# The end of a fused attention and gated-MLP kernel: a residual moved among additions, a projection ordered by tiles, the last tile normalised on VectorE

## The reference, cut to what matters

```python
Q, K, V = x @ wq.T, x @ wk.T, x @ wv.T                       # 64 wide, no softmax
energy  = V^T K summed over the tokens                        # a 64 x 64 matrix
x = layernorm(x + (Q @ energy^T * sqrt(3/64)) @ wo.T)         # 256 wide
h = silu((x @ w1.T) * s1) * ((x @ w2.T) * s2)                 # 1024 wide
h = gelu((h @ h1.T) * hs1)                                    # exact gelu, 1024 x 1024
h = gelu((h @ h2.T) * hs2)                                    # exact gelu, 1024 x 1024
x = layernorm(x + (h @ w3.T) * s3)                            # 256 wide: the output
```

## Time and profile before

| | |
|---|---|
| median of three runs | 668.91 us (667.25 to 669.6) |
| the profiled execution's own time | 669.32 us |
| its span, first to last instruction | 667.5 us |
| TensorE busy | 645.5 us (97%) |
| VectorE busy | 472.5 us (71%) |
| ScalarE busy | 402.9 us (60%) |
| GpSimd busy | 278.1 us (42%) |
| mean granted TensorE clock | 0.989 of full speed |

### The profile page before, as it was taken

How to read it: one execution, slowest core, us unless ns; L and a number is a source line. 1 busy time by engine, 2 the same in 40 slices (tenths; PEclk the granted TensorE clock), 3 DMA queues, 4 the chain that set the end, 5 groups by cost and what they waited for, 6 DMA issues and landing times.

```text
span 667.5 us, 9250 instructions
## 1 busy us (share of the span) xinstructions
PE 645.5 (97%) x3217; PEld 542.1 (81%) x3217; DVE 472.5 (71%) x704; ACT 402.9 (60%) x684; POOL 278.1 (42%) x229
## 2 busy tenths in 40 slices
PE   8988999979999999999999999999999999999994
PEld 6957788858878888888888888888888888888893
DVE  1257557898655799588855799588755799488456
ACT  1366779846764466655764466655764466666663
POOL 0346599569000267059000267059000267078034
PEclk9999999979999999999999999999999999999997
DMA  8999896944340005734340015734340015444101
GB/s 314 402 363 316 325 367 237 358 184 142 135 167 1 1 14 184 275 127 141 133 169 1 1 19 179 275 127 143 135 163 1 0 24 193 162 144 172 64 1 65
DMA packets 24370, 103.89 MB, mean 156 GB/s; under 512 B 2224, under 2 KB 3312, under 8 KB 16496
## 3 DMA queue, kind: packets, MB, share of 16 engines
q1 hardware_dynamic: 24320, 103.24, 43.9%
HBM read 87.51 MB, written 23.07 MB: 166 GB/s over the span
## 4 chain that ended last, share of the span: by engine, by line
PE 82%; POOL 6%; DMA 4%; DVE 3%; ACT 3%; issue 2%; SPq 1%; POOLq 0%; ACTq 0%; DVEq 0%
PE ps L1219 55%; PE ps L1167 17%; PE ps L1277 8%; DMA w_dram<-in_w2T 2%; DMA w<-w_dram 1%; ACT junk L541 1%; PE ps L1106 1%; POOL quarter L496 1%; POOL quarter L499 1%; POOL beside L424 1%; POOL unit L426 1%; POOL unit L428 1%; POOL unit L430 1%; PE ps L1094 1%; ACT R L627 1%
## 5 line engine op out<-in xcount | busy, mean ns | idle before, releaser
L1219 PE MATMUL ps<-R,ring 128*128 128x512 f32 x1792 | 412.0, 391 | 2.2 <-issue 1.3
L1219 PEld LDWEIGHTS ps<-R,ring 128*128 128x128 f32 x1792 | 337.0, 189 | 73.2 <-issue 2.0
L869 DVE TENSOR_TENSOR R<-quarter,R 128x512 fp32r<-128x512 f32 x284 | 256.4, 924 | 68.5 <-ACT R L627 68.2
L627 ACT CAST R<-quarter 128x512 fp32r<-128x512 f32 x288 | 175.5, 616 | 27.1 <-POOL quarter L499 10.0
L1167 PE MATMUL ps<-x1T,w 128*128 128x512 f32 x512 | 119.7, 392 | 2.3 <-DVE quarter L863 2.0
L1167 PEld LDWEIGHTS ps<-x1T,w 128*128 128x128 f32 x512 | 95.3, 188 | 24.5 <-DVE quarter L863 2.4
L673 ACT ACTIVATE quarter<-U,sc 128x512 f32<-128x512 f32 x96 | 69.5, 724 | 71.8 <-DVE U L888 31.6
L477 POOL TENSOR_TENSOR quarter<-quarter,quarter 128x512 f32<-128x512 f32 x32 | 49.4, 1543 | 99.8 <-ACT quarter L673 92.1
L435 POOL TENSOR_TENSOR ve<-mv,eps 128x4 f32<-128x4 f32 x14 | 5.2, 371 | 197.8 <-DVE mv L846 197.8
L593 ACT ACTIVATE sg<-ps,sc 128x512 f32<-128x512 f32 x64 | 44.1, 690 | 66.2 <-PE ps L1167 66.0
L643 ACT COPY U<-ps 128x512 f32<-128x512 f32 x96 | 56.2, 586 | 39.8 <-PE ps L1219 39.7
(11 more groups left out here) (74 smaller groups left out, 344.9 us busy)
## 6 DMA issues: line engine op xcount, KB each, us to landing
ring<-combos SPq DMA_DIRECT2D x56, 1024.0 KB, 4.9
combos<-unit SPq DMA_DIRECT2D x8, 1024.0 KB, 6.3
unit<-in_h1T SPq DMA_DIRECT2D x4, 1024.0 KB, 15.2
xr<-in_x_rows SPq DMA_DIRECT2D x8, 512.0 KB, 5.7
unit<-in_h2T SPq DMA_DIRECT2D x4, 1024.0 KB, 6.9
xT<-in_xT SPq DMA_DIRECT2D x7, 512.0 KB, 8.1
out<-xr SPq DMA_DIRECT2D x7, 512.0 KB, 2.9
w<-w_dram SPq DMA_DIRECT2D x3, 1024.0 KB, 9.4
```

Source lines behind the costliest of these rows:

```text
L627: nc.scalar.copy(R[slot_of(p, u)][:, 0, c, :], quarter[operand_home(p, u)][:, c, :]).then_inc(hi_done, 1)
L869: nc.vector.tensor_tensor(r[:, 1, c, :], quarter[operand_home(p, u)][:, c, :], r[:, 0, c, :].bitcast(f32), ALU.subtract).then_inc(lo_done, 1)
L1219: last = nc.tensor.matmul(ps[:, bank + j, :], w, view(R[slot_of(p, u)][:, part, k, :]), start=n in (0, 1, 5) and k == 0 and part == 0, sto ...
```

## The change

1. VectorE: `residual2(6)` moves ahead of `add_third` 0 in the last hidden layer. `stats` of block 6 is split: bn_stats of tiles 0 and 1 behind add 0, bn_stats of tiles 2 and 3 and all four bn_aggr behind add 1 (ahead of lo 0).
2. TensorE: block 7's 64 matmuls are ordered by tile. With (use, tile): (16,0), (16,1), (16,2), (17,0), (16,3), (17,1), (17,2), (17,3), eight matmuls each. The waits for the additions are set at each tile that needs one, and the four `lo_tail` waits all stand in (16,0), the four `lo_done` waits of use 17 all in (17,0).
3. The last tile of block 7 is normalised by VectorE, as (y - mean) * rstd in one instruction; GpSimd makes no shift for it, and its store waits for the new semaphore `last_norm`.
4. GpSimd makes the shift of block 7's other tiles in one instruction (mean * rstd * -1) in place of two with a wait between them.

```diff
# SyncE
             for q in range(TPB):
-                sp.wait_ge(tile_norm[1], q + 1)
+                sp.wait_ge(*((tile_norm[1], q + 1) if q < TPB - 1 else (last_norm, 1)))
# GpSimd
+            def shift_of_block():
+                nc.gpsimd.tensor_tensor(shift[:, 0, :], mv[1][:, 0, :, 0], nones[:, :], ALU.mult).then_inc(shift_half, 1)
+                pool.wait_ge(shift_half, 1)
+                pool.wait_ge(rstd_done[1], NB - 1)
+                nc.gpsimd.tensor_tensor(shift[:, 0, :], shift[:, 0, :], rstd[1][:, 0, :], ALU.mult).then_inc(shift_done, 1)
+            def shift_of_tile(q):
+                pool.wait_ge(tile_rstd[1], q + 1)
+                nc.gpsimd.tensor_scalar(shift[:, 1, q:q + 1], mv[1][:, 1, q, 0:1], rstd[1][:, 1, q:q + 1], -1.0,
+                                        ALU.mult, ALU.mult).then_inc(shift_done, 1)
...
-                    if ln == 1:
-                        shift_of(slice(q, q + 1), 1, q + 2)
+                    if ln == 1 and q < TPB - 1:
+                        shift_of_tile(q)
# ScalarE
-            for q in range(TPB):
+            for q in range(TPB - 1):
                 normalise_tile(NB - 1, q, q + 2, tile_norm[1])
# VectorE, in the hidden layers
+                if l == 1 and not more:
+                    residual2(NB - 2)
                 for j in range(KH + 1):
...
                     if j < KH:
                         add_third(L, j)
+                    if l == 1 and not more and j < 2:
+                        stats(1, NB - 2, NB - 1, (range(2), range(2, TPB))[j])
# VectorE, in normalised_tilewise
                 if ln == 0:
                     for q in range(early, TPB):
                         normalise_tile(q)
+                else:
+                    normalise_tile(TPB - 1)
...
-            residual2(NB - 2)
-            stats(1, NB - 2, NB - 1)
             normalised_tilewise(1, NB - 1, down_residual, 1)
# TensorE
+            def w3_last(view):
+                p, L = NP - 1, 2 * NP - 1
+                def tile(u, q):
+                    first = u == 16
+                    slot, at = R[slot_of(p, u)], KH if first else 0
+                    if first:
+                        pe.wait_ge(*((gelu_done, n_gelu(L, 1, 2 + q)) if q < 2 else (add_done, n_add(L, 2, q - 2))))
+                    for k in range(KH):
+                        if q == 0:
+                            pe.wait_ge(*((lo_tail, k + 1) if first else (lo_done, n_split(p, 16, k))))
+                        for part in range(2):
+                            last = nc.tensor.matmul(tail_rows(q), view(slot[:, part, k, q * P:(q + 1) * P]), view(w3[:, at + k, :]),
+                                                    start=first and k == 0 and part == 0, stop=not first and k == KH - 1 and part == 1,
+                                                    skip_group_check=True)
+                    if not first:
+                        last.then_inc(w3b, 1)
+                for u, q in ((16, 0), (16, 1), (16, 2), (17, 0), (16, 3), (17, 1), (17, 2), (17, 3)):
+                    tile(u, q)
...
-                        w3_half(NB - 1, 0, view)
-                        w3_half(NB - 1, 1, view)
+                        w3_last(view)
```

More of the change, by code:

```diff
@@ L195, in build @@
         norm_done = [sem(f"norm_done{i}") for i in range(2)]
-        tail_norm = sem("tail_norm")
+        tail_norm, last_norm = sem("tail_norm"), sem("last_norm")
         tile_scaled = sem("tile_scaled")
@@ L526, in _ @@
                 inverse_deviation(1, 2 * p + 1)
-            shift_of(slice(0, TPB), 0, 1)
+            shift_of_block()
             inverse_deviation_tilewise(1)
@@ L831, in residual2, with stats @@
                                         ALU.add).then_inc(sum_done[1], 1)
-            def stats(ln, b, n):
+            def stats(ln, b, n, tiles=range(TPB)):
                 y = xr[:, b % 4, :].rearrange("p (t e) -> p t e", e=E)
@@ L840, in stats @@
                     dve.wait_ge(tile_norm[0], TPB)
-                for q in range(TPB):
+                for q in tiles:
                     last = nc.vector.bn_stats(st[ln][:, b % 2, q, :], y[:, q, :])
+                if tiles[-1] < TPB - 1:
+                    return
                 last.then_inc(stats_done[ln], 1)
@@ L969, in normalise_tile @@
                     nc.vector.tensor_scalar(y[:, q, :], y[:, q, :], mv[ln][:, ln, q, 0:1], rstd[ln][:, ln, q:q + 1],
-                                            ALU.subtract, ALU.mult).then_inc(tile_norm[ln], 1)
+                                            ALU.subtract, ALU.mult).then_inc(tile_norm[0] if ln == 0 else last_norm, 1)
                 for q in range(TPB):
@@ L1259, in w3_half @@
                         pe.wait_ge(gelu_done, n_gelu(2 * p + 1, 1, j))
[L1260 to L1275, removed]
+                for k in range(KH):
+                    pe.wait_ge(lo_done, n_split(p, u, k))
+                    w = view(w3[:, at + k, :])
+                    for q in range(TPB):
                         for part in range(2):
-                            last = nc.tensor.matmul(tail_rows(q) if b == NB - 1 else rows_of(b)[:, q, :], view(slot[:, part, k, q * P:(q + 1) * P]), w,
-                                                    start=first and k == 0 and part == 0 and (q % 2 == 0 or b == NB - 1),
+                            last = nc.tensor.matmul(rows_of(b)[:, q, :], view(slot[:, part, k, q * P:(q + 1) * P]), w,
+                                                    start=first and k == 0 and part == 0 and q % 2 == 0,
                                                     stop=not first and k == KH - 1 and part == 1, skip_group_check=True)
-                    if tail:
-                        last.then_inc(w3b, 1)
                 if u == 15:
@@ L1285, in w3_half @@
                     last.then_inc(w3c, 1)
-                if u == 17 and not tail:
+                if u == 17:
                     last.then_inc(w3b, 1)
+            def w3_last(view):
[5 more added lines that the diff above has]
+                        pe.wait_ge(*((gelu_done, n_gelu(L, 1, 2 + q)) if q < 2 else (add_done, n_add(L, 2, q - 2))))
+                    for k in range(KH):
+                        if q == 0:
[8 more added lines that the diff above has]
+                    tile(u, q)
             pe.wait_ge(zeros_made, 1)
```

## The result

| | before | after |
|---|---|---|
| median of 14 runs | 668.88 us (667.18 to 672.88) | 665.93 us (664.32 to 667.25) |
| ratio, after to before | | 0.9952, 95% interval 0.9937 to 0.9967 |
| profiled span | 667.5 us | 664.4 us |
| first matmul of product 6 (L1219, now L1231) | 642.55 | 642.32 |
| end of the last normalisation | 665.35 | 662.20 |

The change gains 2.95 us by the medians; 2.86 were forecast (665.93 measured, 666.05 predicted). By the interval of the ratio the gain is between 2.2 and 4.2 us. The two executions shown already differ by 0.23 us ahead of product 6, where nothing was changed, so from here on times with a plus sign count from the first matmul of product 6. By that clock the last normalisation ended at +22.80 us before and ends at +19.88 us after, and the span at +24.95 and +22.08.

What follows compares the result with a forecast made beforehand. VectorE's serial queue plus a chain of small steps was taken to bound the end. Last bn_aggr at 661.15, plus 1.34 and 2.15, gives 664.64 against 667.50, 2.86 less; from the median 668.91 that is 666.05 us, range 664.8 to 667.9.

Steps and rivals of the forecast that it cites:

- What bounds it: End of the kernel: VectorE's serial queue plus a chain of small steps; VectorE time lost ahead of 661.44 comes off one for one.
- Part 1: Block 6's residual and statistics moved on VectorE: 4.16 us of work, 1.85 us of cover; lo 3 runs 1.17 us later.
- rival C: VectorE's queue, 644 to 650: all moved work ahead of lo 0 held beside GpSimd; slower, 670.1 us; chance 0.04.
- A (no hold): Waits at operands shared by GpSimd and VectorE don't arise; lo 3 ends 652.9 to 653.5, total 665.3 us; chance 0.22.
- B (further holds): More moved VectorE work held, or slow shift and store landing: gain 1.5, 667.4 us; chance 0.16 together with D.
- Rival D: Tile (16,0) on TensorE waits for `lo_tail` 3 if L444 ends after 650.4; each further 0.5 costs 0.5; 0.16 with B.
- Part 2: Last projection by tiles: TensorE stands 0.90 us for lo 3, first tile ready at 654.81; new order costs 0.4 us.
- Parts 3 and 4: Last tile's steps and GpSimd's shift: 1.34 us from last bn_aggr to normalisation's end in place of 2.39, a gain of 1.05.
- The sum: Whole change: span ends at 664.64 against 667.50, 2.86 us less; from the median, 666.05 us.

Runs made afterwards that it cites:

- e2: Kernel before with only TensorE's new order of the last 64 matmuls; last normalisation at +22.80 us as before, ratio to before 1.0000.
- e1: Kernel before with only block 6's residual and statistics moved; last normalisation at +20.17 us against +22.80, ratio to before 0.9954.
- e6: Full change, but GpSimd's four L444 wait until block 6's residual sum is written; sum takes 1.23 us, last normalisation at +19.89 against +19.88.
- e4: Full change with the old order of the 64 matmuls; last normalisation at +19.53 us against the full change's +19.88, ratio to before 0.9949.
- the repeat: The full change run once more against the kernel before; last normalisation again at +19.88 us, ratio to before 0.9967.
- e5: Full change with tile (16,3) put behind (17,2); last normalisation at +19.41 us against the full change's +19.88, ratio to before 0.9953.
- e7: Full change with block 6's later statistics spread into gaps of VectorE; last normalisation at +19.17 us against the full change's +19.88, ratio to before 0.9952.
- e3: Kernel before with only VectorE's last-tile normalisation and the one-instruction shift; last normalisation at +21.82 us against +22.80, ratio to before 0.9978.

## Why the prediction was right

Step by step, in the prediction's order; predicted times are its own less the 0.23 us by which this execution was ahead.

- **What bounds it.** VectorE's queue ahead of the first tile set the end. e2 shows that TensorE's order alone is worth nothing, e1 that the move is worth 2.63 us of 2.92.
- **Part 1.** The sum L836 was to be held until GpSimd's first instruction ends: about 1.85 us, measured 1.87; lo 0 about 1.35, measured 1.36; lo 3 to end at 653.87, measured 653.88. The bn_stats and additions beside GpSimd were charged nothing, and took 0.74 us a pair and 0.68, against rival C. e6 turns the cause on and off. Rivals A (no hold) and B (further holds) fall with these rows. Rival D's wait for `lo_tail` did not arise: the last L444 ended at 649.32, 0.8 us ahead of need; e6 shows what it looks like when it does.
- **Part 2.** The stop at chunk 3 of (17,0) was put at 0.90 us and cost 0.84 (8.67 - 7.83). It was worked out for the weight load, taken to run 0.22 us ahead of its matmul; after the wait both are recorded at 653.93, so the 31st matmul itself is only 0.73 late, and the 34 from there take 4.34 us, 0.11 more than 30 (3.75) and four more at 0.12. The tiles came 0.08 to 0.11 us earlier than forecast. That the new order costs 0.4 us was forecast and is 0.35 (e4).
- **Parts 3 and 4.** The steps took 1.35 us against 1.34 forecast. The shift that no row had shown took 0.26 us (0.37 in the first tile), inside the bounds given. Two readings were not right. GpSimd was to have 0.6 us of slack for the last tile, and had none to speak of: its rstd instruction took 0.83 and 0.82 us in the middle tiles in place of 0.55 (see the last section), and its last shift ended at 660.94, as the last tile's step was due at 660.93. A tile took GpSimd 1.44 us (659.49 to 660.93) where 1.1 was forecast, against VectorE's 1.45. It cost nothing: GpSimd began 0.08 us after the bn_aggr, as it did in the first tile, when it was idle (656.04 to 656.12). And of the 1.05 us that the prediction books under the last steps, 0.41 are the move's: in e1 GpSimd takes up the last tile 0.11 us after its bn_aggr, not 0.52, with the old shift still in place. By then the steps are worth 0.64 us.
- **The sum.** 2.86 us forecast, 2.92 by the traces up to the last normalisation (2.87 to the end of the span), 2.95 by the medians. The traces bear out the terms; that the medians come within 0.1 us is luck, as their interval is 2 us wide and the repeat gave 2.05 (668.33 - 666.28).

## What to carry to other kernels

Read from the end which engine's queue is late when the slowest engine hands over, and move what does not depend on the handover into that engine's idle time; but count what queues behind it and what a second engine on the same memory is doing there. An order of tiles helps only if it is no earlier than its operands and keeps the tiles closer together than the consumer takes for one; here the order that was added cost 0.35 us, and the better one (e5) gained those back and 0.12 more. e7's 0.71 us came from putting the statistics into waits that VectorE had anyway. e7's statistics with the old order were not run. Compare traces from a fixed point just ahead of the change.

## What the runs showed of the hardware

- **An instruction of VectorE with two SBUF operands waits for GpSimd's running one, and the reverse.** L836 took 1.87 us beside L444 and 1.23 with GpSimd idle (e6); L877 took 1.36 to 1.52 in place of 0.69; L444 took 2.28 in place of 1.30 behind L836. By the rule of the Trainium skill named in the prediction ("SBUF — State Buffer", section "SBUF: two separate sides") this is a lock for a whole instruction; e6's rows agree.
- **GpSimd's small rstd instruction takes 0.55 us or 0.83, by its phase.** It is 0.56 where it starts with VectorE's L1004 (one operand in PSUM, 656.38 and 656.39 after the change) and 0.83 where it starts with L1006 (two SBUF operands, 658.31 and 658.30). Before the change the phases were others and it was 0.55 to 0.56 in all four tiles; there it was the shift (L452) that met the addition (L992) and took 0.43 in place of 0.19 (660.46 and 660.41). It looks like the same hold: in the full change, e1 and e3 every lengthened rstd ends 0.40 to 0.43 us after the addition's end. No run was made to separate it.
- **The spread between traced executions arises in the first 225 us.** Product 6 starts between 639.42 (e2) and 644.00 us (e7) in kernels that do the same up to there. GpSimd's L437 marks the way: it starts at 52.18 in e2 and 54.09 in e7, later at 220.00 and 224.56, and at 546.60 and 551.16, so the difference is 1.91, 4.56 and 4.56 us. Two stretches of each (stretch, its length, busy time of TensorE, its weight loads, VectorE, ScalarE and GpSimd, clock, DMA share, GB/s), first e2:

```profile
0.00:60.00 60.00, 56.47 (x352) 46.81 (x353) 22.72 (x52) 27.39 (x47) 20.26 (x33) 1.00 0.98 367
...
120.00:180.00 60.00, 56.43 (x259) 46.31 (x259) 50.37 (x77) 42.16 (x73) 30.96 (x23) 0.97 0.56 196
```

Then e7:

```profile
0.00:60.00 60.00, 54.56 (x344) 45.24 (x345) 22.41 (x51) 25.61 (x44) 18.24 (x32) 1.00 0.96 359
...
120.00:180.00 60.00, 56.24 (x253) 45.98 (x252) 51.40 (x75) 42.07 (x73) 34.08 (x25) 0.94 0.59 211
```

The granted clock was lower in e7 from 120 to 180 us, but the first 1.91 us arose where it was 1.00 in both. What makes the two differ was not studied.
